# First stage of an AdaLN block: statistics taken two units ahead in halves, normalisation in halves

## The reference, cut to what matters

```python
def _layernorm(x, axis=-1, eps=1e-05):
    m = jnp.mean(x, axis=axis, keepdims=True)
    v = jnp.var(x, axis=axis, keepdims=True)
    return (x - m) / jnp.sqrt(v + eps)
...
    h = _layernorm(x, axis=-1) * (1 + ca) + sa
...
        qkv = x @ w_qkv
...
        Q = apply_rope(Q)
        K = apply_rope(K)
```

## Time and profile before

| what | before |
|---|---|
| median of 3 runs | 3191.26 us (3191.11 to 3191.93) |
| the profiled execution's own time | 3209.92 us |
| its span, first to last instruction | 3208.1 us |
| busy share of the span: TensorE, VectorE, ScalarE, GpSimd | 90%, 79%, 50%, 28% |
| instructions | 61398 |
| first stage, first rotation to the last third part | about 43 to 287 us of the span |
| TensorE's granted clock, units 1 to 15 of the first stage | full |
| TensorE's granted clock, 284 to 380 us | half |

### The profile page before, as it was taken

One profiled execution on the slowest core, in us unless ns is written; L12 is line 12 of the kernel. 1 busy time (PEld: TensorE's weight loads), 2 busy tenths in 40 slices (PEclk: granted clock), 3 DMA queues, 4 the chain that ended last, 5 costly groups with the idle time before them and its releaser, 6 DMA issues. The chain is left out here.

```text
span 3208.1 us, 61398 instructions
## 1 busy us (share of the span) xinstructions
PE 2873.9 (90%) x22508; PEld 1604.1 (50%) x22508; DVE 2522.7 (79%) x4693; ACT 1590.9 (50%) x2160; POOL 894.0 (28%) x1101
## 2 busy tenths in 40 slices
PE   6885699999999999999999997875699999989998
PEld 3553123333333333333333322764588888878887
DVE  5885998888988889888988870676577777767887
ACT  2442076666666666666666676332344444412111
POOL 5774011111111110111101112477222222244453
PEclk9997599999999999999999999986899999999999
DMA  4776201221112211112112101774654555333342
GB/s 130 214 200 190 70 25 49 56 54 41 45 49 53 57 38 47 49 51 58 35 49 52 49 8 43 218 231 162 204 158 154 158 159 159 120 99 124 99 125 79
DMA packets 388532, 317.91 MB, mean 99 GB/s; under 512 B 112721, under 2 KB 374845, under 8 KB 388289
## 3 DMA queue, kind: packets, MB, share of 16 engines
q1 hardware_dynamic: 368640, 275.57, 29.8%
q0 software_dynamic: 12288, 33.57, 3.2%
q10 hardware_dynamic: 7360, 5.51, 0.6%
HBM read 196.89 MB, written 116.93 MB: 98 GB/s over the span
## 5 line engine op out<-in xcount | busy, mean ns | idle before, releaser
L918 ACT ACTIVATE probs<-ps_s 128x1024 f32<-128x1024 f32 (+3 forms) x1280 | 1078.0, 896 | 599.4 <-PE ps_s L1086 598.9
L941 DVE TENSOR_REDUCE piece_rest<-ps_m 128x1 f32<-128x512 f32 (+2 forms) x1260 | 748.9, 647 | 91.6 <-PE ps_m L1061 42.0
L898 POOL TENSOR_SCALAR_AFFINE_SELECT probs<-probs 128x256 f32<-128x256 f32 x512 | 206.0, 409 | 1480.8 <-ACT probs L918 1475.7
L1086 PE MATMUL ps_s<-q_st,k_st 50*128 50x512 bf16 (+7 forms) x5120 | 594.6, 346 | 19.0 <-ACT probs L918 15.2
L1101 PE MATMUL ps_o<-probs,vs 128*32 128x512 f32 (+3 forms) x5120 | 600.9, 541 | 4.4 <-POOL probs L898 1.2
L941 DVE TENSOR_REDUCE piece_late<-ps_m 128x1 f32<-128x512 f32 x900 | 549.0, 666 | 33.4 <-PE ps_m L1053 17.4
L1053 PE MATMUL ps_m<-k_st,q_st 48*128 48x512 bf16 (+3 forms) x2400 | 407.6, 353 | 65.8 <-DVE piece_rest L941 48.0
L1053 PEld LDWEIGHTS ps_m<-k_st,q_st 48*128 48x128 bf16 x2400 | 106.8, 93 | 651.6 <-DVE piece_rest L941 338.9
L1086 PEld LDWEIGHTS ps_s<-q_st,k_st 50*128 50x128 bf16 (+1 forms) x5120 | 224.2, 95 | 251.0 <-ACT probs L918 91.0
L1857 ACT ACTIVATE act_g<-ps_g 128x512 f32<-128x512 f32 x117 | 70.1, 599 | 279.4 <-PE ps_u L1959 279.4
L2135 ACT ACTIVATE act_g<-ps_g 128x512 f32<-128x512 f32 x80 | 47.9, 599 | 278.8 <-PE ps_u L2232 238.4
(11 more groups left out here) (230 smaller groups left out, 5123.9 us busy)
## 6 DMA issues: line engine op xcount, KB each, us to landing
k_st<-qk_parts SPq DMA_DIRECT2D x768, 32.0 KB, 1.8
qk_parts<-parts SPq DMA_DIRECT2D x124, 192.0 KB, 2.8
q_st<-qk_parts SPq DMA_DIRECT2D x720, 32.0 KB, 1.8
x_r<-expert_rows SPq DMA_DIRECT2D x39, 512.0 KB, 4.5
expert_made<-made SPq DMA_DIRECT2D x39, 512.0 KB, 3.0
x_in<-in_L_attn_x_dram SPq DMA_DIRECT2D x32, 512.0 KB, 4.8
vs<-v_ones SPq DMA_DIRECT2D x64, 256.0 KB, 3.7
v_ones<-v_out SPq DMA_DIRECT2D x60, 256.0 KB, 4.7
```

What stands on the lines that cost most here:

```text
L898: pool.affine_select(out=block_now, in_=block_now, compare_op=ALU.is_ge, fill=0.0, base=0, pattern=[[0, 2], [1, P]], channel_multiplier=-1 ...
L918: act.activation(probs[:, u % PSLOTS, 2 * pair:2 * pair + 2, j * P:ST], ps_s[:, pair, :, j * P:ST], ACT.Exp, scale=SCALE).then_inc(exp_don ...
L941: v.tensor_reduce(dst, ps_m[:, bank, 0:n * w].rearrange("p (n w) -> p n w", n=n), AX.X, ALU.max) \
L1086: last = pe.matmul(ps_s[:, pair, z, j * P:ST], k_st[rows, slot, half, pair, kc * P:(kc + 1) * P], q_st[rows, slot, half, pair, qt * ST + j ...
```

## The change

`run` gets a function `has` in place of the flag `more`: `has(k)` says whether there is a unit k ahead. The pass ahead of the first unit becomes two. VectorE's `stat` takes a `half`: its first two tiles in step 2 and the other two with the aggregation in step 3, both for unit u + 2. `normalise` takes a `half` too: the first two tiles in step 0, the others and the wait in step 1, for unit u + 1. Both now stand behind the subtraction of their step. GpSimd's `rstds` moves to the end of step 3, for unit u + 2. The first `run` below is GpSimd's, the second VectorE's.

```diff
-        for u in range(-1, SPB):
-            run(u // SPB, u % SPB, within(u)(1), around(u // SPB, u % SPB, within(u)))
+        for u in range(-2, SPB):
+            run(u // SPB, u % SPB, within(u), around(u // SPB, u % SPB, within(u)))
...
             def run(b, s, has, tile):
                 for t in range(TPS):
                     if tile(t, 0):
                         add(b * SPB + s, t)
-                    if t == 0 and more:
-                        rstds(b * SPB + s + 1)
                     if tile(t, 3):
                         u, tt, slot, _ = tile(t, 3)
                         third(u, tt, slot)
+                    if t == 3 and has(2):
+                        rstds(b * SPB + s + 2)
...
-            def stat(u, slot, turn):
+            def stat(u, slot, turn, half):
                 v.wait_ge(x_loaded[slot], turn * 16)
-                for t in range(TPS):
+                for t in range(half * (TPS // 2), (half + 1) * (TPS // 2)):
                     last = v.bn_stats(stats[:, t, :], x_in[:, slot, t, :])
+                if half == 0:
+                    return
                 last.then_inc(dve_own, 1)
...
-            def normalise(u, slot, x_slot):
+            def normalise(u, slot, x_slot, half):
                 v.wait_ge(rstd_done, u + 1)
-                for t in range(TPS):
-                    ins = v.tensor_scalar(xn[:, slot, t, :], x_in[:, x_slot, t, :], mv[:, t, 0:1], rstd[:, t:t + 1],
-                                          ALU.subtract, ALU.mult)
-                    ins.then_inc(xn_done, 1)
-                v.wait_ge(xn_done, (u + 1) * TPS)
-                v.sem_inc(x_read, 1)
+                for t in range(half * (TPS // 2), (half + 1) * (TPS // 2)):
+                    v.tensor_scalar(xn[:, slot, t, :], x_in[:, x_slot, t, :], mv[:, t, 0:1], rstd[:, t:t + 1],
+                                    ALU.subtract, ALU.mult).then_inc(xn_done, 1)
+                if half == 1:
+                    v.wait_ge(xn_done, (u + 1) * TPS)
+                    v.sem_inc(x_read, 1)
...
             def run(b, s, has, tile):
                 for t in range(TPS):
                     if tile(t, 0):
                         rope(b * SPB + s, t, s * TPS + t)
-                    if t == 0 and more:
-                        stat(b * SPB + s + 1, (s + 1) % SPB, b + ((s + 1) // SPB + 1))
                     if tile(t, 3):
                         u, tt, slot, _ = tile(t, 3)
                         leave(u, tt, slot)
-                    if t == 1 and more:
-                        normalise(b * SPB + s + 1, (s + 1) % 2, (s + 1) % SPB)
+                    if t < 2 and has(1):
+                        normalise(b * SPB + s + 1, (s + 1) % 2, (s + 1) % SPB, t)
+                    if t >= 2 and has(2):
+                        stat(b * SPB + s + 2, (s + 2) % SPB, b + ((s + 2) // SPB + 1), t - 2)
```

More of the change, by code:

```diff
@@ L335, in within @@
             return lambda k: 0 <= u + k < NST
-        for u in range(-1, SPB):
-            run(u // SPB, u % SPB, within(u)(1), around(u // SPB, u % SPB, within(u)))
+        for u in range(-2, SPB):
+            run(u // SPB, u % SPB, within(u), around(u // SPB, u % SPB, within(u)))
         with engine.Fori(1, B - 1) as b:
             for s in range(SPB):
-                run(b, s, True, around(b, s, lambda k: True))
+                run(b, s, lambda k: True, around(b, s, lambda k: True))
         for u in range((B - 1) * SPB, NST + 1):
-            run(u // SPB, u % SPB, within(u)(1), around(u // SPB, u % SPB, within(u)))
+            run(u // SPB, u % SPB, within(u), around(u // SPB, u % SPB, within(u)))
     with ExitStack() as ctx:
@@ L488, in third, with run @@
                                    parts[:, slot, 1, :, t * P:(t + 1) * P], ALU.subtract).then_inc(part3, 1)
-            def run(b, s, more, tile):
+            def run(b, s, has, tile):
                 for t in range(TPS):
@@ L595, in second, with run @@
                     .then_inc(part2, 1)
-            def run(b, s, more, tile):
+            def run(b, s, has, tile):
                 for t in range(TPS):
-                    if t == 2 and more:
+                    if t == 2 and has(1):
                         modulate(b * SPB + s + 1, (s + 1) % 2, b + (s + 1) // SPB)
```

## The result

The changed kernel takes 3197.23 us (median of 15 runs, 3192.80 to 3199.55); the kernel before, run beside it, 3191.46 (15 runs, 3186.74 to 3196.71). The ratio is 1.0016, 95% interval 1.0009 to 1.0024: 0.16% slower, where 18 us or 0.57% faster was forecast. The profiled execution took 3196.73 us. That of the kernel before was 18.5 us above its median, and as much lies behind the first stage (from unit 15 to the end of the span 2937.8 us, against 2919.1 in the changed kernel's profile), so the two profiles are compared in the first stage alone.

What follows compares the result with a forecast made beforehand. Two TensorE stalls over a 12.95 us floor bound a unit; 15.25 to 14.05 saves 1.20, so 16.8 in units 1 to 14 plus 1.2 in unit 0: 3191.26 - 18.0 = 3173.3 us, range 3160 to 3185.

Steps and rivals of the forecast that it cites:

- two stalls of TensorE: Units 1 to 14: q and k transposes wait 13.0 us for VectorE's subtraction, h transposes 10.4 for normalised rows.
- The rule for a held normalisation: VectorE's normalisation meeting a running GpSimd instruction ends about 0.15 us after it; back-to-back GpSimd instructions each hold one.
- GpSimd's pair: GpSimd's two small instructions making 1/std, queued after addition and subtraction at tile 3; done 2.16 us into the next unit.
- The late x: Rival at tile 2: statistics wait for x's load; if all loads took 10.1 us, 15 us lost, 3206; chance 0.05.
- The step that failed: VectorE at tile 0: first normalisation meets GpSimd's small instruction, second its addition, ending at 3.58; next rotation at 3.50 us.
- the dearer one: Upper bound on normalisation time: first half meets GpSimd's addition and subtraction; tile 0 3.98, unit 14.53, 0.72 us saved.
- stall for `rest`: TensorE's q and k transposes at tile 2: needed subtraction allows 5.57, before their natural 5.83 us, so the wait is gone.
- no wait of the transposes of q and k: Sign expected in the changed trace: these TensorE transposes never wait for `rest` in units 1 to 14.
- a unit above 15: Sign in the changed trace: a unit longer than 15 us makes the prediction, 14.05, wrong.
- The dearer case: Rival at tile 0: first half of the normalisations meets two long GpSimd instructions; 11 us saved, 3180; chance 0.15.
- Nothing moves: Rival: stall of h transposes grows by what the other gives back, or stores hold attention's start; 3188 to 3194; chance 0.09.
- the dearest reading of the rows: Latest end allowed for the fourth normalisation in the unit: 8.03 us, against the 8.75 needed for no gain.

Runs made afterwards that it cites:

- experiment 6: Changed kernel with one normalisation per tile, statistics halves at tiles 0 and 1, 1/std at tile 1's end, double-buffered statistics, earlier x load: 3158.94 us, 0.9895 of before.
- experiment 2: Changed kernel with all four statistics at tile 2 and GpSimd's 1/std pair ahead of its addition at tile 3: 3182.33 us, 0.9969 of the kernel before.
- experiment 3: GpSimd's subtraction left out, third parts filled with zero once: 3161.78 us (0.9902) from the changed kernel, 3178.40 us (0.9961) from the one before.
- experiment 4: Four unused transposes in TensorE's wait for the fourth normalised tile: 3191.27 us (0.9993) from the changed kernel, 3195.57 us (1.0015) from the one before.
- experiment 1: Changed kernel with all four normalisations together at tile 1 again, statistics still two units ahead: 3176.34 us, 0.9949 of the kernel before.

## Why the prediction was wrong

**What held.** What bounds the kernel (two stalls of TensorE, 2.3 us a unit, over a floor of 12.95): experiment 6 removes both and lands on 12.95. The rule for a held normalisation, and the addition and subtraction of GpSimd as what holds it: experiments 2 and 3. Tiles 1, 2 and 3: 4.36, 3.13, 3.06 foreseen, 4.37, 3.14, 3.06 measured. Unit 0: 1.09 saved (13.55 to 12.46), 1.2 foreseen. GpSimd's pair done 2.16 into the unit: 2.13 measured (137.98 - 135.85). The late x: no wait for it in the changed kernel.

**The step that failed** is the first item of the working in the next unit: "Tile 0: first normalisation at 1.87 meets the small instruction until 2.16, ends at 2.31; the second, ready at 2.23, finds the addition". That small instruction makes the 1/std which this normalisation needs. It could not be ready at 1.87; it is ready when the result has come, 2.19, and GpSimd's next instruction is by then under way, so that each of the two normalisations goes behind one long instruction, not one of them. Tile 0 takes 4.64 for 3.50. The prediction had the time of the result right and treated its consumer as a bystander. Its unit was 14.05; with 4.64 in place of 3.50 the same sum gives 15.19, and most units measure 15.1 to 15.2. The text weighed what the pair itself waits for (it "holds up nothing behind it"), and did not ask who waits for the pair. Neither bound held it either: the dearer one, 14.53, still let the first normalisation start at 1.87; experiment 2 shows that case. From the same step comes the stall for `rest`, which the prediction called gone: its own sum with tile 1 starting 1.14 later puts those transposes at 6.71, behind their natural 5.83. They came at 6.72. Of the signs that the prediction listed, "no wait of the transposes of q and k" failed, and its last, a unit above 15, came.

**What the prediction did not have at all** is the clock. The gain that was left, 1.2 us in units 1 to 14 without the falls (213.50 against 212.31) and 1.1 in unit 0, would have made the kernel about 2 us faster; experiment 4, at 0.9993, agrees, though its interval reaches 1.0002. The clock's falls cost 1.7 us in each of units 3, 4, 12 and 13 (17.23, 16.42, 16.78 and 16.78 against 15.53, 14.74, 15.09 and 15.09 with the four transposes), 6.8 together. In the profiled executions the first rotation also starts 1.07 later than before; such starts lie between 43.1 and 44.6 in the kernels without experiment 3's filling (43.8 and 43.1 in the two profiles of experiment 1's kernel), so the difference is not put down to the change. The first stage as a whole: 1.07 - 1.09 + 5.50 = 5.5 us later, against 5.8 by the medians.

**The rivals.** The dearer case has the mechanism of tile 0 but for the dependence, the late x is the only one with the right sign, and it was not the cause. "Nothing moves" was set aside since the fourth normalisation would have to end at 8.75 and the dearest reading of the rows gave 8.03. It ended near 8.70: 144.86 less the 0.30 of the wait is 144.56, 8.71 after R0. The reading was not the dearest, since it left the dependence out. So in what it says of the units this rival, at a chance of 0.09, came nearest; the time of the changed kernel lies above its 3188 to 3194 by the clock.

**Still open**: why the clock falls in four of the units and not in the others, which have the same two waits. The runs show only that the waits 2 us apart come before all four falls (products of q and k at 96.37, 113.09, 236.83 and 253.31), that filling 0.43 us of the second prevents it, and that two waits 2.1 apart of which the first is 0.26 long (experiment 2) brought no fall in one profiled execution. The changed kernel was profiled once, so that its other executions have four falls too is inferred from the medians. Open as well is what tile 0 would take if the first normalisation did not need 1/std and yet came while the pair ran: the 3.50 of the forecast is a case that no run could make.

## What to carry to other kernels

When work is moved to an earlier place, write down for each of its inputs when it is made in the new order, before asking what resource it meets: here the producer stood on another engine, right ahead of the two instructions that then held the consumer. Where two engines take turns at a port, put the instructions that need it one at a time behind work that does not need it, rather than in a run. Two short waits of TensorE cost here more than their lengths once they stood near each other, though not in every unit: compare the granted clock, stretch by stretch, before a time is explained by the waits alone.

## What the runs showed that I had not expected

TensorE's granted clock falls to half for some 3.4 us out of a stretch in which it is 90% busy (196.63 of 219.00 us), behind two waits of 0.7 and 0.8 us whose ends are 2.0 us apart; four transposes in the second wait, 0.43 us of work that nobody uses, make a kernel some 7 us faster. The same four cost 4.7 us where the clock had not fallen. Where the hardware loop is entered (behind unit 3) and where it goes round (behind unit 7), tile 3 takes 3.5 us in place of 3.06 if VectorE has no slack there; behind unit 11, where the loop is left, it takes 3.11. Tile 0 of units 4 and 8 is shorter by about the same.
